# A decoder layer on one core: the order of work where cross-attention hands over to the FFN

## What is computed

```
x = x + rwkv_attention(layernorm(x))                  # time mixing and a scan over 128 tokens
x = x + cross_attention(layernorm(x), ctx, mask)      # 16 heads; the delta is layer-normed again
x = x + ffn(layernorm(x))                             # 512 -> 2048 -> 512

def bitlinear(x, w, b):                               # used twice in ffn, exact Gelu between
    xn = layernorm(x)                                 # xc * rsqrt(var + 1e-5)
    s  = 127 / max(abs(xn)) ;  xq = round(xn * s) / s
    ws = mean(abs(w))       ;  wq = clip(round(w / ws), -1, 1) * ws
    return xq @ wq.T + b
```

## Time and profile before

| | |
|---|---|
| median of 3 executions | 1006.79 us |
| lowest, highest | 1006.04, 1010.59 us |
| the profiled execution: its time, its span | 1009.11 us, 1007.3 us |
| busy, share of the span: TensorE, VectorE, ScalarE, GpSimd | 90%, 78%, 49%, 15% |
| mean granted TensorE clock | 0.947 of 2.4 GHz |

### The profile page before, as it was taken

One profiled execution on the slowest core, in us unless ns is written; L12 is line 12 of the kernel. 1 busy time (PEld: TensorE's weight loads), 2 busy tenths in 40 slices (PEclk: granted clock), 3 DMA queues, 4 the chain that ended last, 5 costly groups with the idle time before them and its releaser, 6 DMA issues.

```text
span 1007.3 us, 18914 instructions
## 1 busy us (share of the span) xinstructions
PE 910.0 (90%) x7673; PEld 736.6 (73%) x7690; DVE 789.0 (78%) x1205; ACT 488.6 (49%) x687; POOL 147.1 (15%) x210
## 2 busy tenths in 40 slices
PE   3467999999989999999999999999999956989996
PEld 1457988888888889889989778878888723445552
DVE  4878878779787797878658576889888779789983
ACT  4435253352534525344152434455444334979994
POOL 3000111021110211102020200000000032334331
PEclk9589999999999999999997999999999967999999
DMA  9320102011020110202313032221332132123220
GB/s 247 113 76 14 44 11 95 12 33 64 11 95 12 32 64 12 74 12 96 105 41 128 7 121 106 87 85 81 125 125 84 64 97 62 63 84 95 95 74 32
DMA packets 36951, 72.47 MB, mean 72 GB/s; under 512 B 6466, under 2 KB 7234, under 8 KB 35850
## 3 DMA queue, kind: packets, MB, share of 16 engines
q1 hardware_dynamic: 35754, 68.29, 20.5%
q0 software_dynamic: 1120, 3.10, 1.2%
HBM read 57.76 MB, written 12.58 MB: 70 GB/s over the span
## 4 chain that ended last, share of the span: by engine, by line
PE 59%; issue 16%; DVE 14%; POOL 5%; DMA 2%; ACT 2%; SPq 1%; DVEq 0%; POOLq 0%; ACTq 0%
PE S L674 11%; PE P L62 7%; PE P L63 6%; PE P L64 6%; PE S L2139 4%; PE P L2129 4%; PE S L650 3%; POOL sm L370 3%; DVE E L1732 2%; DVE xf L919 2%; PE S L1593 2%; PE P L627 1%; PE S L1547 1%; PE S L1595 1%; POOL rsf L385 1%
## 5 line engine op out<-in xcount | busy, mean ns | idle before, releaser
L674 PE MATMUL S<-R,K 64*128 64x64 f32 x1792 | 117.7, 283 | 5.1 <-DVE K L965 2.8
L674 PEld LDWEIGHTS S<-R,K 64*128 64x128 f32 x1792 | 110.2, 196 | 16.2 <-issue 10.9
L370 POOL TENSOR_TENSOR sm<-sm,mhalf 128x16 f32<-128x16 f32 x8 | 30.6, 3826 | 280.5 <-DVE sm L1012 280.5
L2129 PE MATMUL P<-wq,xqT 128*128 128x512 bf16 x240 | 66.0, 397 | 3.6 <-DMA w1b<-b1p 1.5
L2139 PE MATMUL S<-wq,hqT 128*128 128x512 bf16 x255 | 62.9, 394 | 5.0 <-ACT hqT L2072 5.0
L919 DVE TENSOR_TENSOR xf<-P,xx 128x1024 f32<-128x1024 f32 x40 | 48.9, 1222 | 19.4 <-PE P L627 19.3
L1732 DVE TENSOR_SCALAR E<-S,upper 128x2048 f32<-128x2048 f32 x16 | 37.6, 2349 | 28.7 <-PE S L1580 28.5
L1738 DVE RECIPROCAL rec<-S 128x512 f32<-128x512 f32 x16 | 53.6, 3351 | 4.5 <-PE S L1595 4.3
L962 DVE TENSOR_TENSOR R<-R,D 128x256 f32<-128x256 f32 x96 | 40.9, 426 | 18.1 <-PE S L674 16.5
L1406 ACT ACTIVATE E<-E 128x2048 f32<-128x2048 f32 x16 | 30.6, 1913 | 41.9 <-DVE E L1732 41.9
L2139 PEld LDWEIGHTS S<-wq,hqT 128*128 128x128 bf16 x256 | 25.2, 101 | 33.9 <-ACT hqT L2072 5.1
(11 more groups left out here) (284 smaller groups left out, 2723.0 us busy)
## 6 DMA issues: line engine op xcount, KB each, us to landing
wch<-in_wff SPq DMA_DIRECT2D x32, 256.0 KB, 3.6
cwch<-in_wff SPq DMA_DIRECT2D x8, 1024.0 KB, 6.6
xt<-in_x SPq DMA_DIRECT2D x8, 512.0 KB, 4.5
y<-in_x SPq DMA_DIRECT2D x8, 512.0 KB, 3.8
out<-y SPq DMA_DIRECT2D x8, 512.0 KB, 3.4
cxt<-out SPq DMA_DIRECT2D x8, 512.0 KB, 4.2
ct<-in_ctx SPq DMA_DIRECT2D x8, 512.0 KB, 5.1
cxr<-out SPq DMA_DIRECT2D x8, 512.0 KB, 6.7
```

The lines of the kernel that those rows point to most:

```text
L370: pool.tensor_tensor(sm[:, 2, :], sm[:, 1, :], mhalf[:, 0:2 * H], ALU.pow).then_inc(y_rstd, 1)
L674: mm = pe.matmul(ps[:, par, b, k, :], K[head_rows(par), r % 2, T * g:T * g + T], right_tokens(par, g, i), start=True, stop=True)
L2129: pe.matmul(Hp[:, cols], xqT[t % 2][:, k, :], w1q[:, k, cols], start=k == 0, stop=False)
```

## The change

It reorders instructions at the seam; none is added or left out. The waits that guard the FFN's opening loads and GpSimd's clearing of w1b change from "the last pair's V is projected" to "its Q has been copied out" and, on GpSimd, also "its context is split".

```
 SyncE, cross_parts.finish
-            step(None, PAIRS - 1, PAIRS - 2, PAIRS - 3)
+            load_ternary(PAIRS - 2)
+            load_residual(PAIRS - 3)
             load_ternary(PAIRS - 1)
-            sp.wait_ge(v_done, PAIRS)
+            sp.wait_ge(q_ready, NC * PAIRS)
             sp.wait_ge(x_turned, PAIRS)
             sp.wait_ge(cl_ready, PAIRS)
             f["open"]()
             f["rows"]()
-            for n in range(2, 4):
-                f["step"](n)
+            store(PAIRS - 3)
+            sp.wait_ge(v_done, PAIRS)
+            f["step"](2)
             load_residual(PAIRS - 2)
+            f["step"](3)
             store(PAIRS - 2)

 GpSimd, cross_parts.finish
             run_to_last(pool, step)
-            pool.wait_ge(v_done, PAIRS)
+            pool.wait_ge(q_ready, NC * PAIRS)
+            pool.wait_ge(cl_ready, PAIRS)
             f["open"]()
             f["step"](0)
             step(None, None, PAIRS - 1, PAIRS - 2)
-            for n in range(1, 4):
-                f["step"](n)
+            f["step"](1)
+            f["middle"](0)
+            f["front"](2)
+            f["step"](3)

 ScalarE, cross_parts.finish
             attend(last, 0)
+            attend(last, 1)
             normalize_delta(last - 1)
-            attend(last, 1)
...
             f["center"](1)
+            f["square"](1)
             copy_delta(last)
             f["copy_x"](2)
             f["copy_h"](0)
-            f["square"](1)
             f["step"](4)

 VectorE, cross_parts.rest
             clip(last, 0)
             last_stats(last - 1)
+            clip(last, 1)
             last_norm(last - 1)
-            clip(last, 1)
             f["step"](1)
             attended(last, 0)
             attended(last, 1)
+            f["middle_variance"](0)
+            f["middle"](0)
             low(last, os_, o[:, :, :, :].rearrange("p k b t -> p (k b t)"), oh_ready, ol_ready)
+            f["middle_scale"](0)
+            f["front"](2)
             last_gain(last - 1)
             add_last(last - 1)
-            f["step"](2)
             f["step"](3)
```

More of the change, by code:

```diff
@@ L1994, in gpsimd, with front @@
     def gpsimd(pool):
+        def front(f):
+            pool.wait_ge(s_var, f + 1)
+            pool.tensor_tensor(s1[f % 2][:, 0:1], s1[f % 2][:, 1:2], fmhalf[:, 0:1], ALU.pow).then_inc(s_pow1, 1)
+            if f == 0:
+                pool.wait_ge(s_zero, 3)
+                pool.wait_ge(s_unit, 2)
+            pool.wait_ge(s_xrec, f + 1)
+            if f >= 2:
+                pool.wait_ge(s_p_turned, f - 1)
+            pc, pr = pieces[f % 2], pres[f % 2]
+            pool.tensor_tensor(pr[:, 0:1], s1[f % 2][:, 3:4], inv_w1[:, :], ALU.mult).then_inc(s_inv, 1)
+            for i in range(3):
+                if i == 0:
+                    pool.wait_ge(s_inv, f + 1)
+                else:
+                    pool.wait_ge(s_pres, 2 * f + i)
+                pool.tensor_copy(pc[:, 3 * i:3 * i + 3], wide(pr[:, i:i + 1], [P, 3])).then_inc(s_piece, 1)
+                if i < 2:
+                    pool.wait_ge(s_piece, 3 * f + i + 1)
+                    pool.tensor_tensor(pr[:, i + 1:i + 2], pr[:, i:i + 1], pc[:, 3 * i:3 * i + 1], ALU.subtract).then_inc(s_pres, 1)
@@ L1995, in step, with middle @@
+        def middle(m):
+            pool.wait_ge(s_var2, m + 1)
+            pool.tensor_tensor(s2[m % 2][:, 3:4], s2[m % 2][:, 2:3], fmhalf[:, 0:1], ALU.pow).then_inc(s_pow2, 1)
+            if m == 0:
+                pool.wait_ge(biases_in, 16)
+            pool.wait_ge(xr_in[m % 2], 16 * (m // 2 + 1))
+            if m >= 2:
+                pool.wait_ge(s_out, m - 1)
+            pool.tensor_tensor(xb[m % 2][:, :], xr[m % 2][:, :], b2[:, :], ALU.add).then_inc(s_xb, 1)
         def step(f, t, m, b, o):
@@ L1996, in step @@
             if f is not None:
[L1997 to L2016, removed]
@@ L2017, in step @@
-            if m is not None:
[L2018 to L2025, removed]
+                front(f)
@@ L2027, in open_early @@
+            if m is not None:
+                middle(m)
         def open_early():
@@ L2044, in rest @@
                 step(*turns(n))
-        return {"open": open_early, "step": lambda n: step(*turns(n)), "rest": rest}
+        return {"open": open_early, "front": front, "middle": middle, "step": lambda n: step(*turns(n)), "rest": rest}
     def scalar(act):
@@ L2248, in step, with front_whole @@
                 middle_scale(m)
+        def front_whole(f):
+            front(f)
+            front_inverse(f)
+            front_scale(f)
         def open_early():
```

12 lines of the change are left out of this document (7 added, 5 removed).

## The result

| | before | after |
|---|---|---|
| median of 4 executions, same chip | 1007.98 us | **995.24 us** |
| lowest, highest | 1006.04, 1010.59 | 994.79, 996.44 |
| ratio, 95% interval | | 0.9874 [0.9847, 0.9901] |
| span of the profiled execution | 1007.3 us | 993.8 us |
| mean granted TensorE clock | 0.947 | 0.953 |

What follows compares the result with a forecast made beforehand. The seam (800 to 866 us) was taken as bound by waits, the late FFN by TensorE. Terms 1 and 2 (9.3) plus term 3 (5.1) sum to 14.4, from 1006.79 to 992.4 us; range 990 to 997.5.

Steps and rivals of the forecast that it cites:

- Term 1: VectorE before the last chunk's quantize: loading chunk 7 earlier removes the wait for it, -6.9 us.
- Terms 1 and 2: Seam up to attended: earlier chunk, first product no longer held by bias rows; attended at 819.6 instead of 828.95, -9.3 us.
- rival 1: Bias rows late, GpSimd held beside VectorE: 0.7 us lost, 993.1; with another 4 us of slow loads 997.1; chance 0.07.
- The exponentials ahead of the norm: ScalarE: Exp(7,1) ends at 816.3, early enough for the weighing; norm and table load follow, Gelu(0) may start at 819.1.
- Term 3: First Gelu row ahead of pair 6's residual: VectorE's waits for high half and second square go, -1.1 - 4.0 = -5.1 us.
- Rival 2: A hidden second bound (store order, missed wait) sets the seam's end; under 5 us come, 1002 to 1009; chance 0.05.
- Rival 3: Slower: short TensorE bursts keep the 1.2 GHz clock into the FFN's rows; two rows cost 18.4 us, about 1011; chance 0.03.
- my ends: Clock ends of the forecast: full clock throughout 990.8 us; half level through product and weighing 997.2; with the forecast, chance 0.82.
- TensorE-bound, carried whole: After the first output row: order unchanged and TensorE-bound, so the whole 14.4 us gain is kept to the end.
- The sum: Seam's gains added: 9.3 + 5.1 = 14.4 us, VectorE at 851.4 instead of 865.79, forecast 992.4 us.

Runs made afterwards that it cites:

- All but the exponentials: The changed kernel with only attend and clip of (7,1) put back behind the norm; 994.92 us, ratio 0.9848 to the kernel before.
- the late residual: The changed kernel with two delta buffers, pair 6's residual behind VectorE's FFN step 3, copy_delta before the second square, FFN step 4 issued earlier; 992.18, then 991.89 us.

## Why the prediction was right, and where it was off

- **Term 1, the chunk: right.** The quantize starts at 799.91 behind the residual without idle time, where the chunk's wait of 6.91 stood.
- **Terms 1 and 2, -9.3 at attended: right.** Measured are 9.29 between the two traces (828.95 to 819.66), 9.2 counted from pair 5's residual. The steps hold too: b1c landed at 793.5 (forecast 795.1), the rows were issued by 800.7 (forecast 804.3) and ahead of the product (rival 1 fell: GpSimd's five operations, early now, took 0.20 to 0.22 each), scores(7,1) at 809.50 (809.7), the product from 811.92 to 817.65 (811.8 to 817.6).
- **The exponentials ahead of the norm: costed rightly at no gain of their own.** All but the exponentials is at 20.88 and 53.80, as the change. For the table load my row did not settle a second cost; this trace does. The load ends at 818.66 and Gelu(0) starts at 818.68. The Trainium skill's drain of about 1.38 us ("ScalarE: Activation LUTs", What ACT_TABLE_LOAD costs) isn't seen here, neither behind the load nor ahead of it, where ScalarE's norm ends at 817.36 and the load begins at 817.38.
- **Term 3, -5.1: mis-sized, it brought 3.9.** Both waits named, 1.12 and 4.03, went as forecast, and the term fails in the sentence on what would be late next: "row 0's transposes (up to 1.9), a product of 5.8 and the second product with row 3's transposes (about 4.3) end near 849.4, 2 us before row 0's output is wanted". I let TensorE go straight from the projection, which ended at 835.8 (forecast 837.4), to row 0's transposes. What stands between is row 2's turning, which needs GpSimd's pieces, and they now fall beside pair 6's residual: 3.52 us. I had named that interference for the bias rows, up to 803.7, and did not ask where else GpSimd now meets a VectorE operation with two SBUF inputs. The clock fell to 0.50. VectorE was ready for xo at 850.85, 0.5 us before the forecast, and then waited 1.72, so that xo came at 852.57 and not 851.4. The copy of the last delta, which waits for the residual to free d, I missed too; undone alone it brought 0.39 us.
- **Rival 2 in small.** "A second bound, a missed wait" was given 0.05 and a loss of over 9 us; what came was such a wait, priced at 1.72.
- **Rival 3 fell.** The clock was low from 808 to 816 and 840 to 848 and, for a moment, behind 880; no row was lost to it. But its cost in the first stretch is larger than my ends allowed for the better side: with the full clock from 804 to 820, xo came 2.7 us earlier and not 1.6.
- **"TensorE-bound, carried whole": carried, but for another reason.** From xo to the span's end it took 141.5 us before and 141.2 after. TensorE isn't what carries it up to row 6: there it waits 2.79 us for VectorE before, 2.78 after, so it is VectorE's unchanged list that takes the gain on (27.78 us from xo to row 6 in both).
- **The sum.** 14.4 less the 1.2 of term 3 is 13.2, beside 13.1 at xo and 13.5 in the span. The prediction of 992.4 was 2.8 too low, of which 1.2 is that step. Another 1.2 is the base: the kernel before gave 1007.98 this time where I had started from 1006.79. The 0.4 left lie between 13.1 at xo and 12.7 between medians, less than a measurement can tell. Terms 1 and 2 came to within 0.1 us. Of term 3's wait of 1.72 us, 0.5 was made good because VectorE's list was shorter than summed, and that part was luck.

## What to carry to other kernels

When work is moved ahead of a wait, look at what the *small* engines do at its new place: five short operations on GpSimd took 4.4 us from first to last instead of 1.5 (835.99 to 840.38, and 835.93 to 837.46 with the late residual), and held TensorE's queue, because VectorE's operations with two SBUF inputs now ran beside it. When a buffer is single, list its next writer before the move. And where TensorE has short bursts ahead of a critical stretch, a few matmuls that compute nothing can pay for themselves (2.7 us here for eight); price the slow clock over the whole stretch, and not over the one product, and look where it falls next. Two gains that both shorten waits of one engine for another need not add up: here the second brought 0.2 us in the traces.

## What was not expected of the hardware

- GpSimd's operations on 128x1 and 128x3 took 0.19 us alone and 1.05 to 1.20 beside VectorE's product and additions of 128x1024 with both inputs in SBUF, each ending with one of those. Moving these away brought them back to 0.19.
- Eight matmuls of 128x512, some 2 us of work, kept the clock at 1.00 where it had been 0.52 and 0.62 for 8 us; it fell to 0.85 and 0.72 from 820 to 828 instead.
- Gelu started 0.02 us after its table load of 1.28 us.
